# Reciprocal roots of two token stages taken from ScalarE to GpSimd

## The reference

```
x = x + conv_branch_0(ln_c(x))                 # the branch ends in a 1x1 projection
t = tokens(x); t = t + ffn_0(ln_t(t)); x = image(t)
x = x + conv_branch_1(ln_c(x))                 # ends in a 1x1 projection with a bias
t = tokens(x); t = t + ffn_1(ln_t(t)); x = image(t)

ln(v)  = (v - mean(v)) / sqrt(var(v) + eps)    # over the 48 channels; eps 1e-5 in ln_t, 1e-6 in ln_c
ffn(x) = q16(q16(relu(q16(q16(q8(x) q8(W1)) + q8(b1)))...) with W2, b2)
         # q8 rounds to an 8-bit float (5 exponent bits), q16 to a 16-bit float; 48 -> 192 -> 48
```

## Time and profile before

| | before |
|---|---|
| median of three runs | 2532.38 us (lowest 2532.0, highest 6105.01) |
| the profiled execution | 2536.14 us, span 2534.4 us |
| PE busy | 2148.1 us (85%) |
| DVE busy | 1439.6 us (57%) |
| ACT busy | 1151.7 us (45%) |
| POOL busy | 532.4 us (21%) |

### The profile page before, as it was taken

One profiled execution on the slowest core, in us unless ns is written; L12 is line 12 of the kernel. 1 busy time (PEld: TensorE's weight loads), 2 busy tenths in 40 slices (PEclk: granted clock), 3 DMA queues, 4 the chain that ended last, 5 costly groups with the idle time before them and its releaser, 6 DMA issues. The chain is left out here.

```text
span 2534.4 us, 69339 instructions
## 1 busy us (share of the span) xinstructions
PE 2148.1 (85%) x25034; PEld 1260.1 (50%) x25034; DVE 1439.6 (57%) x2567; ACT 1151.7 (45%) x2290; POOL 532.4 (21%) x912
## 2 busy tenths in 40 slices
PE   7679949998996999999879999999936777688887
PEld 3345517766784333333346666666614545233332
DVE  3345501111112777777657888787834445588887
ACT  4346522222222888888722323232201111477776
POOL 7610007100100000000046565656520000000000
PEclk9789959999997999999989999999968989799999
DMA  6999988777654677878466666666449885344443
GB/s 154 262 256 269 247 295 282 263 264 228 255 216 97 130 150 144 151 141 154 101 113 133 126 134 129 130 129 130 113 112 271 250 247 175 87 112 108 109 110 84
DMA packets 559393, 434.57 MB, mean 171 GB/s; under 512 B 363592, under 2 KB 498432, under 8 KB 555878
## 3 DMA queue, kind: packets, MB, share of 16 engines
q1 hardware_dynamic: 476982, 384.66, 58.0%
q10 hardware_dynamic: 76128, 22.48, 4.4%
q0 software_dynamic: 6128, 25.11, 4.0%
HBM read 247.30 MB, written 188.38 MB: 172 GB/s over the span
## 5 line engine op out<-in xcount | busy, mean ns | idle before, releaser
L615 PE MATMUL gate_ps<-gate_data,gate_wt 64*64 64x289 f32 x6144 | 391.2, 411 | 29.4 <-issue 22.2
L615 PEld LDWEIGHTS gate_ps<-gate_data,gate_wt 64*64 64x64 f32 x6144 | 307.6, 134 | 114.1 <-issue 45.8
L676 DVE TENSOR_TENSOR gate_out<-gate_gelu,gate_ps 128x578 f32<-128x578 f32 x96 | 72.2, 756 | 375.4 <-PE gate_ps L615 327.1
L968 ACT CAST mix_h<-mix_bank 96x512 f16<-96x512 f32 x512 | 267.6, 592 | 10.3 <-PE mix_bank L919 6.4
L2076 PE MATMUL fus_bank<-fus_xt,fus_taps 64*32 64x256 f32 x3840 | 139.9, 422 | 78.1 <-issue 55.0
L653 ACT ACTIVATE gate_gelu<-gate_ps 128x578 f32<-128x578 f32 x96 | 62.7, 653 | 300.7 <-PE gate_ps L615 275.1
L1053 DVE TENSOR_SCALAR mix_hb<-mix_h,mix_b1q 96x1024 f16<-96x1024 f16 x256 | 122.7, 479 | 98.0 <-ACT mix_h L968 98.0
L919 PE MATMUL mix_bank<-mix_xq,mix_w1q 112*96 112x512 fp8e5 x512 | 143.1, 381 | 34.3 <-ACT mix_h L968 23.0
L1063 DVE CAST mix_hq<-mix_hb 96x2048 fp8e5<-96x2048 f16 x128 | 156.5, 1223 | 21.1 <-DVE mix_hb L1053 19.2
L292 DVE COPY exp_out<-exp_y 128x384 f32<-128x384 f32 x192 | 102.3, 566 | 104.3 <-PE exp_y L255 54.1
L255 PE MATMUL exp_y<-exp_win,exp_xb 48*128 48x192 f32 x1024 | 117.8, 368 | 47.8 <-DVE exp_out L292 29.7
(11 more groups left out here) (237 smaller groups left out, 4182.2 us busy)
## 6 DMA issues: line engine op xcount, KB each, us to landing
y<-exp_out SPq DMA_DIRECT2D x64, 816.0 KB, 12.3
gate_data<-y SPq DMA_DIRECT2D x24, 2176.0 KB, 16.7
g<-gate_out SPq DMA_DIRECT2D x48, 578.0 KB, 4.4
mix_sc<-g SPq DMA_DIRECT2D x31, 816.0 KB, 7.2
wav_strips<-xp SPq DMA_DIRECT2D x96, 204.0 KB, 3.5
init<-wav_init SPq DMA_DIRECT2D x48, 272.0 KB, 2.3
fus_init<-init SPq DMA_DIRECT2D x48, 272.0 KB, 6.3
xp<-mix_xn SPq DMA_DIRECT2D x124, 102.0 KB, 2.8
```

Of the source, the lines that this page charges most:

```text
L615: mm = pe.matmul(banks(a, v)[64 * g:64 * (g + 1), r], wt[q][64 * r:64 * (r + 1), 2 * a + g, n, :], src, start=n == 0, stop=n == 3)
L968: act.copy(h16[at.pair][:, m, h, :], bank[(2 * m + h) % len(bank)][0:HID, :]).then_inc(h16_ready, 1)
```

## The change

In `root`, ACT now only adds eps to the variance on its way out of PSUM (`shifted`, an Identity with a bias), and GpSimd raises it to the power of a tile that holds -0.5 (`exponent`), which gives `rstd`. The exponential on ACT goes. ACT's instruction now also waits for the power of two steps before, and the power waits until the product that used its output buffer two steps before is done. `variance("in")` on PE and `root("in")` on ACT move ahead of the hidden layer's pieces in each turn. `normalise` moves from the end of DVE's turn at stage 5 to the place behind `add_residual` at stage 6, and `store_norm` on SP from stage 7 to stage 8.

```diff
-                staged(sp, 2 * N, KEPT, [(0, load), (SHOWN + 1, store_x2)] + [(7, store_norm)] * wide, LEAD)
+                staged(sp, 2 * N, KEPT, [(0, load), (SHOWN + 1, store_x2)] + [(8, store_norm)] * wide, LEAD)
...
-                pieces = [(0, project), (SHOWN, show), (2, hide(0)), (2, hide(1)), (1, variance("in")), (0, centre_in)]
+                pieces = [(0, project), (SHOWN, show), (1, variance("in")), (2, hide(0)), (2, hide(1)), (0, centre_in)]
                 if norm_dst is not None:
-                    pieces = [(0, project), (3, show), (2, hide(0)), (4, centre_out), (2, hide(1)), (1, variance("in")), (5, variance("out")), (0, centre_in)]
+                    pieces = [(0, project), (3, show), (1, variance("in")), (2, hide(0)), (4, centre_out), (2, hide(1)), (5, variance("out")), (0, centre_in)]
...
                         act.wait_ge(var[v], at.n + 1)
-                        act.activation(logv[v][at.pair][:, :], var_bank[v][0:CP, :], ACT.Ln,
-                                       bias=eps[0:CP, m:m + 1]).then_inc(logged[v], 1)
-                        act.wait_ge(logged[v], at.n + 1 + FREE[v])
-                        act.activation(rstd[v][at.pair][:, :], logv[v][at.pair][:, :], ACT.Exp, scale=-0.5).then_inc(rooted[v], 1)
+                        act.wait_ge(rooted[v], at.n + 1)
+                        act.activation(shifted[v][at.pair][:, :], var_bank[v][0:CP, :], ACT.Identity,
+                                       bias=eps[0:CP, m:m + 1]).then_inc(evicted[v], 1)
...
-                pieces = [(SHOWN, round_shown), (2, round_hidden(0)), (2, round_hidden(1)), (1, root("in")),
-                          (0, square("in"))]
+                pieces = [(SHOWN, round_shown), (1, root("in")), (2, round_hidden(0)), (2, round_hidden(1)), (0, square("in"))]
                 if norm_dst is not None:
-                    pieces = [(3, round_shown), (2, round_hidden(0)), (4, square("out")), (2, round_hidden(1)), (1, root("in")), (5, root("out")), (0, square("in"))]
+                    pieces = [(3, round_shown), (1, root("in")), (2, round_hidden(0)), (4, square("out")), (2, round_hidden(1)),
+                              (5, root("out")), (0, square("in"))]
...
+            @block.gpsimd
+            def _(pool):
+                pool.wait_ge(prepared, 1)
+                for v in norms:
+                    pool.sem_inc(rooted[v], 2)
+
+                def power(v):
+                    def piece(at):
+                        pool.wait_ge(evicted[v], at.n + 1 + FREE[v])
+                        pool.wait_ge(xq_ready if v == "in" else xn_ready, at.n + 1)
+                        pool.tensor_tensor(rstd[v][at.pair][:, :], shifted[v][at.pair][:, :], exponent[:, :], ALU.pow
+                                           ).then_inc(rooted[v], 1)
+                    return piece
+
+                staged(pool, 2 * N, KEPT, [(1, power("in"))] + [(5, power("out"))] * wide, LEAD)
...
+                dve.memset(exponent[:, :], -0.5)
...
                 pieces = [(0, add_residual), (SHOWN, add_shown), (2, bias_hidden), (2, quantize_hidden), (1, quantize_norm)]
                 if norm_dst is not None:
-                    pieces.append((5, normalise))
+                    pieces = [(0, add_residual), (6, normalise)] + pieces[1:]
                 staged(dve, 2 * N, KEPT, pieces, LEAD)
```

More of the change, by code:

```diff
@@ L701, in token_mix @@
         center, average = k.sb("center", [CP, CP]), k.sb("average", [CP, CP])
-        eps = k.sb("eps", [128, 2])
+        eps, exponent = k.sb("eps", [128, 2]), k.sb("exponent", [CP, NT])
         proj = k.sb("proj", [HID, C] if wide else [CP, CP])
@@ L724, in token_mix @@
         norms = ("in", "out") if norm_dst is not None else ("in",)
-        sq, logv, rstd = ({v: [k.sb(f"{name}_{v}{u}", [CP, NT]) for u in U] for v in norms}
-                          for name in ("sq", "logv", "rstd"))
+        sq, shifted, rstd = ({v: [k.sb(f"{name}_{v}{u}", [CP, NT]) for u in U] for v in norms}
+                          for name in ("sq", "shifted", "rstd"))
         xq = [k.sb(f"xq{u}", [CP, NT], F8) for u in U]
@@ L744, in token_mix @@
         projected, x1_ready, xq_ready = (k.sem(s) for s in ("projected", "x1_ready", "xq_ready"))
-        centered, squared, var, logged, rooted = ({v: k.sem(f"{s}_{v}") for v in norms} for s in (
-            "centered", "squared", "var", "logged", "rooted"))
+        centered, squared, var, evicted, rooted = ({v: k.sem(f"{s}_{v}") for v in norms} for s in (
+            "centered", "squared", "var", "evicted", "rooted"))
         hidden, h16_ready, hb_ready, hq_ready, mixed, y16_ready, yb_ready, x2_ready, xn_ready = (
@@ L903, in piece @@
                             if isinstance(at.n, int):
-                                pe.wait_ge(logged["out"], at.n + FREE["out"])
+                                pe.wait_ge(evicted["out"], at.n + FREE["out"])
                         pe.wait_ge(squared[v], at.n + 1)
@@ L913, in piece @@
                     def piece(at):
-                        pe.wait_ge(xq_ready, at.n + 1)
+                        pe.wait_ge(xq_ready, at.n + 3)
                         if m == 1 and len(bank) == 2:
@@ L926, in show @@
                     if norm_dst is not None:
-                        pe.wait_ge(logged["out"], at.n + 1)
+                        pe.wait_ge(evicted["out"], at.n + 1)
                     pe.sem_inc(pe_turn, 1)
@@ L944, in _ @@
                 for v in norms:
-                    act.sem_inc(logged[v], FREE[v])
+                    act.sem_inc(evicted[v], FREE[v])
                 act.sem_inc(y16_ready, 1)
@@ L1013, in _ @@
                 dve.sem_inc(xn_ready, 2)
+                dve.sem_inc(xq_ready, 2)
                 def add_residual(at):
@@ L1044, in quantize_norm @@
                 def quantize_norm(at):
-                    dve.wait_ge(rooted["in"], at.n + 1)
+                    dve.wait_ge(rooted["in"], at.n + 3)
                     dve.sem_inc(dve_turn, 1)
@@ L1076, in normalise @@
                 def normalise(at):
-                    dve.wait_ge(rooted["out"], at.n + 1)
+                    dve.wait_ge(rooted["out"], at.n + 3)
                     dve.wait_ge(norm_out[at.pair], 32 * at.block + 32)
```

2 lines of the change are left out of this document (1 added, 1 removed).

## The result

The changed kernel takes 17816 us (median of 4 runs, 17811 to 17825) against 2532 us; the ratio is 7.04, 95% interval 7.03 to 7.06. Slower was forecast and slower it is, but the 3040 us (2700 to 3560) of the forecast are far off. The profiled execution has a span of 17819.3 us.

The account below looks back on a forecast made before the run. It took the new order's ring through DVE, PE and ACT, lengthened by GpSimd's power locking out DVE, to set the turns: 2536 + 476 + 32 + 2 = 3046 us, given as 3040, range 2700 to 3560.

Parts of the forecast that it names:

- What the power costs: GpSimd's power in both token stages: three passes over 512 columns, 2.83 us; from one pass, 1.07, to six, 5.47.
- six passes or more: Rival: a GpSimd power this long sets the turns, 16.7 us in `mix0` and 11.0 in `mix1`, 3520 us; chance 0.25.
- the ring: Both token stages: `add_residual`, `variance("in")`, Identity, roundings, `bias_hidden`, `quantize_hidden`, `quantize_norm`, next `add_residual`; 8.08 us in `mix0`, 7.06 in `mix1`.
- GpSimd decides: Rival in both token stages: powers of six passes or more set the turn, 3520 us; chance 0.25.
- What the new order closes: Sooner `variance("in")` closes a ring of waits in both token stages: turns 1.15 and 1.67 us longer, 181 us.
- Whether it runs beside DVE: GpSimd's power and DVE's SBUF-only instructions exclude each other: turns 4.47 us longer in `mix0`, 2.97 in `mix1`, 476 us.
- the lock: In SBUF, GpSimd's power and DVE's `bias_hidden`, `quantize_hidden` and `add_shown` exclude each other; with three passes chance 0.38, 3040 us.
- the ring alone: Rival: power of about one pass, or no exclusion of DVE's instructions; only the order's ring counts, 2733 us; chance 0.31.
- What is removed: ACT's exponential, 0.69 us, twice a turn in `mix0`, once in `mix1`; gain at most 0.44 and 0.61 us a turn.
- The clock: TensorE's granted clock falls from full to 0.88 in both token stages, costing 32 us.
- The rest: Both token stages: TensorE's clock 32 us, memset under 1 us a stage, new ACT wait and later store costed at nothing.

Follow-up runs that it names:

- the product run: Changed kernel with GpSimd's power replaced by a product of the exponent tile with itself, waits and order kept: 2715.7 us, ratio 1.071.
- The run of the order alone: Kernel before with the change's whole order on PE, ACT, DVE and SP, roots still on ACT as logarithm and exponential: 2805.7 us, ratio 1.106.
- the single root: Kernel before, order untouched, one ACT absolute reciprocal square root in place of logarithm and exponential: 2528.8 us, ratio 0.998.

## Why the prediction was wrong, step by step

- *What the power costs.* This is the step that failed: "I take three passes, 0.19 + 3 x 0.88 = 2.83 us. The far end is six passes, 5.47 us." It costs 82.14 us, the time of 93 such passes; the price goes by columns, and why a column costs 0.160 us no run shows. There was no row of a power, and the far end was no bound at all; it was three functions at the price of one product, doubled. Nothing in the trace limited it from above. The rival "six passes or more" got a chance of 0.25, and yet the range closed a little above six; only the last line, "if a power costs many times six passes", left the case open. With the measured price in the prediction's own links, `mix1` would have come to 82.14 and some 3.4 us from the ring's other links (4.4 at the low clock level), and `mix0` to 2 x 82.14: the 17.8 ms that were measured. The rival "GpSimd decides" named the mechanism, and was sized by the same bound.
- *What the new order closes.* Right, and nearly to the size: 181 us was the ring's sum, the product run shows 182 (2715.7 against 2534.1). That the two agree to 1 us is luck: most turns, 8.0 and 7.0 us, are a little shorter than 8.08 and 7.06, and a few longer ones, in `mix1` at a lower clock, which the sum doesn't hold, make up for it. The run of the order alone, with the exponential inside it, shows 272 against 260. In the changed kernel the ring is hidden in `mix0` and is the 4.4 us between two powers in `mix1`.
- *Whether it runs beside DVE.* Wrong for the power. The cast beside an 82 us power takes 1.22 us, and only the SBUF instructions that start 0.5 to 1.0 us behind the start of a power are longer, and they end by 1.6: 0.74 in place of 0.35 us, 0.64 in place of 0.48. From 1.2 us on nothing is. The rule that the loser is blocked for the whole instruction (the Trainium skill, "SBUF — State Buffer", section "Who interferes with whom") fits the product that waited out the cast, 1.94 against 1.04 us, and doesn't fit the power. Of the 2.97 and 4.47 us a turn in the forecast, 1.67 and 1.15 are the ring's; the other 1.30 and 3.32, 295 us in all, were built on the lock and don't exist. Without them, and with its 2.83 us, the forecast would have been that of the ring alone, 2733.
- *What is removed.* Right that it would bring little: the single root brought 5 us, 10 at most, and no shorter turn (6.93 and 5.39).
- *The clock.* Right in direction. With the order alone `mix1` runs at 0.86 and about one turn in four pays the 0.94 us that I had at 1.03; `mix0` stays at 1.00. With the product `mix1` is at 0.93 and `mix0` at 1.00, where the forecast took 0.88 for both. In the changed kernel the stages are at 0.52 and 0.53, the low level, with PE busy 6% and 8% of the time. There it costs some 64 us by estimate, 4.4 against 3.4 us in each turn of `mix1`, and nothing in `mix0`, where GpSimd sets the turn.
- *The rest.* The store a step later was costed at nothing. Together with `normalise`'s new place it cost 18 us in the old order; in the new order the same move takes 0.60 us a turn out of `mix0`'s ring.

## What to carry to other kernels

An operation that has no row in the trace has no upper bound there either: measure it alone, in one kernel, before anything is rebuilt around it, and until then write the case "many times dearer" with a real chance. Before an engine is relieved, look for what waits on the instruction that goes; here nothing that sets a turn waited on the exponential; PE's projection waited on the logarithm in front of it. And when a piece is moved sooner in one engine's order, list the waits it takes along: a shared PSUM bank turned a late, free wait into a ring through three engines.

## What the runs showed of the hardware

- GpSimd's elementwise power costs 0.160 us a column of float32, whatever the rows (1 to 112) and with either exponent tried; a product or a sum of 112 x 512 takes 1.04 to 1.50 us, a power of it 82.1 to 83.4.
- While it runs it leaves VectorE alone but for its start: 16-bit instructions in SBUF that began 0.50 to 1.04 us behind it took 0.15 to 0.47 us longer, one that began 1.23 us behind it did not. Why was not looked at. Products that read PSUM and began 0.07 to 0.43 us behind it kept their 0.69 us.
- A GpSimd product that starts 0.19 us behind a VectorE cast from 16 to 8 bits waits it out (1.94 us in place of 1.04), and the cast loses nothing.
- ScalarE's absolute reciprocal square root takes 0.69 us on 112 x 512 out of PSUM, as the logarithm does.
